# One order for 64 attentions: S0, S1, S2, C0, S3, C1, ..., C29, C30, C31, in a decoder layer on one NeuronCore

## What is computed

```python
x1 = layernorm(x + self_attention(x))         # 16 heads of 16, rotary embedding, no mask
x2 = layernorm(x1 + cross_attention(x1, ctx)) # 16 heads of 16, key mask, biases, out projection
gates = softmax(x2 @ router_w + router_b)     # 8 experts, top 2
```

## Time and profile before

| | us |
|---|---|
| median of 3 runs | 2200.92 (2197.92 to 2202.95) |
| the profiled execution | 2197.93 |
| its span in the profile | 2196.1 |
| h0 begins, h4 begins | 15.58, 102.42 |
| h61 begins | 1442.89 |
| last product with the values (C31) ends | 1577.02 |
| first matmul on rows of experts | 1606.36 |

### The profile page before, as it was taken

The page is one execution under the profiler, slowest core; times in us unless marked ns, Lnnn a source line. Parts: engine busy times, 40 slices in busy tenths (PEclk is TensorE's granted clock), DMA queues, the critical chain, the costliest instruction groups (busy, mean ns, idle before and its releaser), DMA issues. The chain is left out here.

```text
span 2196.1 us, 48374 instructions
## 1 busy us (share of the span) xinstructions
PE 2151.0 (98%) x18871; PEld 1498.1 (68%) x18877; DVE 1197.1 (55%) x2512; ACT 992.4 (45%) x1514; POOL 653.8 (30%) x1011
## 2 busy tenths in 40 slices
PE   8999999999999999999999999999999999999996
PEld 4566666666666666666666666666567877778785
DVE  3566776676776766776766776764411111111146
ACT  2355555555555555555555555555212122222233
POOL 2122233333233333233333233333221212121244
PEclk7899999999999999999999999999999999999998
DMA  3330101111100110000100000100023224331353
GB/s 109 101 114 31 36 32 50 55 43 52 53 27 27 36 34 30 28 22 25 31 31 27 28 24 23 33 29 19 13 60 80 39 63 89 80 73 32 84 209 158
DMA packets 96288, 117.01 MB, mean 53 GB/s; under 512 B 11360, under 2 KB 89005, under 8 KB 94016
## 3 DMA queue, kind: packets, MB, share of 16 engines
q1 hardware_dynamic: 66640, 82.37, 11.5%
q0 software_dynamic: 17184, 19.66, 4.9%
q10 hardware_dynamic: 12240, 11.88, 1.6%
HBM read 65.84 MB, written 56.05 MB: 56 GB/s over the span
## 5 line engine op out<-in xcount | busy, mean ns | idle before, releaser
L877 DVE TENSOR_REDUCE smax<-ps_s 128x4 f32<-128x1024 f32 x500 | 610.0, 1220 | 303.5 <-PE ps_s L577 264.0
L763 ACT ACTIVATE prob<-ps_e 128x1024 f32<-128x1024 f32 x500 | 512.0, 1024 | 497.6 <-PE ps_e L586 397.4
L577 PE MATMUL ps_s<-stack 17*128 17x256 f32 x4000 | 571.3, 403 | 14.8 <-DVE smax L877 9.1
L586 PE MATMUL ps_e<-stack 18*128 18x256 f32 x4000 | 567.6, 401 | 1.1 <-ACT prob L763 1.0
L577 PEld LDWEIGHTS ps_s<-stack 17*128 17x128 f32 x4000 | 346.6, 185 | 195.7 <-issue 104.1
L586 PEld LDWEIGHTS ps_e<-stack 18*128 18x128 f32 x4000 | 341.9, 184 | 5.9 <-issue 4.2
L1668 ACT ACTIVATE hid<-m_ps_h,b_sb 128x320 f32<-128x320 f32 x256 | 134.7, 527 | 392.2 <-PE m_ps_h L1622 392.2
L1622 PE MATMUL m_ps_h<-m_cols,w_sb 128*128 128x320 f32 x1024 | 290.7, 433 | 0.6 <-DVE m_cols L1691 0.6
L1639 PE MATMUL m_ps_o<-w_sb,hid 128*128 128x256 f32 x1280 | 279.1, 379 | 1.0 <-DVE m_res L1720 1.0
L1639 PEld LDWEIGHTS m_ps_o<-w_sb,hid 128*128 128x128 f32 x1280 | 243.1, 190 | 36.2 <-DVE m_res L1720 1.4
L602 PE MATMUL ps_w<-prob,val 128*32 128x256 f32 x4096 | 253.6, 389 | 0.2 <-ACT prob L763 0.2
(11 more groups left out here) (147 smaller groups left out, 2289.5 us busy)
## 6 DMA issues: line engine op xcount, KB each, us to landing
w_sb<-in_w SPq DMA_DIRECT2D x16, 1024.0 KB, 6.1
slot_rows_dram<-m_rows ACTq DMA_DIRECT2D x40, 258.0 KB, 2.6
m_rows<-slot_rows_dram SPq DMA_DIRECT2D x15, 645.0 KB, 4.2
xT<-in_xT SPq DMA_DIRECT2D x32, 256.0 KB, 2.8
ctxT<-in_ctxT SPq DMA_DIRECT2D x32, 256.0 KB, 2.8
x_res<-in_x SPq DMA_DIRECT2D x32, 256.0 KB, 2.7
sums_dram<-x SPq DMA_DIRECT2D x32, 256.0 KB
c_rows<-sums_dram SPq DMA_DIRECT2D x8, 1024.0 KB, 14.0
```

Of the source, the lines that this page charges most:

```text
L577: mm = nc.tensor.matmul(scores[:, p % 2, t, :], stack[X][rows, Q, p // HG, t * P:(t + 1) * P], stack[X][rows, K, p // HG, :], start=True, ...
L586: mm = nc.tensor.matmul(shifted[:, p % 2, t, :], stack[Y][rows, K, h // HG, t * P:(t + 1) * P], stack[Y][rows, Q, h // HG, :], start=True, ...
L763: nc.scalar.activation(prob[:, h:h + 2, :].rearrange("p h s -> p (h s)"), shifted[:, :, :, :].rearrange("p h t s -> p (h t s)"), ACT.Exp, ...
L877: nc.vector.tensor_reduce(max_columns(X, p), scores[:, :, :, :], AX.X, ALU.max)\
```

## The change

The 64 attentions get one written order, `items`, and half step h is: scores of item h, shifted scores of item h-1, output of item h-2, preparation of item h+1, and x2 and routing of a cross item at h-3 and h-4. Nothing is left out between the first and the last item, so there are 65 half steps with duos, 63 of them with two streams (h0 has S0's scores alone, h64 C31's shifted scores alone). S(b) comes at h(2b-2) from b = 3 on, C(b) stays at h(2b+3) up to C29, and C30 and C31 follow it at h62 and h63.

```diff
+        items = [(SELF, 0), (SELF, 1), (SELF, 2)]
+        for b in range(NB - 3):
+            items += [(CROSS, b), (SELF, b + 3)]
+        items += [(CROSS, NB - 3), (CROSS, NB - 2), (CROSS, NB - 1)]
+        rank = {item: k for k, item in enumerate(items)}
...
+        def side(at_item):
+            return rank[at_item] % 2
+        def fellow(at_item):
+            return item(rank[at_item] - 2)
...
+        def half_steps(emit, eng):
+            for h in range(2 * NB + 4):
+                emit(h, item(h), item(h - 1), item(h - 2), item(h + 1), item(h - 3), item(h - 4))
...
+        OUT_ROWS, X2_COLUMNS, COUNT, PROJECT_OUT, ROUTE, VALUES, EARLY_VALUES = 1, 3, 5, 6, 6, 7, 1
+        COLUMNS, STACK_K, STACK_Q = (4, 5), (5, 6), (6, 7)
+        LATE_STACK_K, LATE_STACK_Q = (6, 6), (7, 7)
+        PROJECT, LATE_PROJECT = ((2, 2, 3, 3), (2, 3, 5, 5)), ((3, 3, 4, 4), (3, 3, 5, 5))
...
-            spins_beside_one_stream = {
-                (last + 1, CROSS): (0, (0, 0, 2, 3, 3, 0, 0, 0)), (last + 2, SELF): (2, (2, 2, 3, 2, 0, 2, 1, 2)),
-            }
+            spins_beside_one_stream = {2 * NB: (2, (2, 2, 3, 2, 0, 2, 1, 2))}
...
+                    if s is not None and early(s) and m == EARLY_VALUES:
+                        values(*s, 0)
+                        values(*s, 1)
...
-                    n = (2 * i + X - 1) * DUOS + m
-                    if 0 <= n < EMPTY_PARTS:
-                        empty_rows(n)
+                    k = (h - 2) * DUOS + m
+                    if 0 <= k < EMPTY_PARTS:
+                        empty_rows(k)
...
+                settled = item(h - 5)
+                if is_of(CROSS, settled) and settled[1] < NB - 3:
+                    scatter(settled[1])
...
+                if is_of(CROSS, r):
+                    if p != (CROSS, NB - 1):
+                        place(r[1])
+                    if r[1] >= NB - 3:
+                        scatter(r[1])
```

More of the change, by code:

```diff
@@ L514, in project @@
                     take_bank("project", Y, b, half)
+                if n == 0 and Y == CROSS and b == 0:
+                    pe.wait_ge(load_w.sem, load_w.count(0))
                 if n == 0:
@@ L617, in columns @@
                 take_bank("columns", X, b)
-                rows = x1 if X == SELF else att2
+                rows = x1[b % 2] if X == SELF else att2
                 for k in range(KD):
@@ new lines, in emit @@
+                    if n is not None and m == slot_of(STACK_Q, LATE_STACK_Q, n):
+                        make_stack("stack_q", *n, 0)
+                    if is_of(CROSS, q) and m == ROUTE:
+                        route(q[1])
+                    if s is not None and not early(s) and m == VALUES:
+                        values(*s, 0)
+                        values(*s, 1)
+                    if h in spins_beside_one_stream:
+                        w, times = spins_beside_one_stream[h]
+                        if times[m] and w in held:
+                            steps_of, at_b, at_k = held[w]
+                            pe.wait_ge(steps_of.sem, steps_of.count(at_b, at_k))
+                        keep_warm(times[m], ps_w[:, w, :])
@@ L723, in _ @@
+                    if (h, m) in spins:
+                        pe.wait_ge(s_max[CROSS].sem, s_max[CROSS].count(NB - 1))
+                        pe.wait_ge(e_exp[CROSS].sem, e_exp[CROSS].count(NB - 1))
+                        keep_warm(spins[h, m])
             for n in range(4):
@@ L747, in stack_columns @@
                 act.wait_ge(tr_mm[Y].sem, tr_mm[Y].count(b, 2 * half + (1 if part == K else 2)))
-                if part == K and e_mm[Y].due(b - 1, 4 * half + 4):
-                    act.wait_ge(e_mm[Y].sem, e_mm[Y].count(b - 1, 4 * half + 4))
-                nc.scalar.copy(stack[Y][:, part, 2 * half:2 * half + 2, :],
+                other = fellow((Y, b))
+                if part == K and other is not None:
+                    act.wait_ge(e_mm[other[0]].sem, e_mm[other[0]].count(other[1], 4 * half + 4))
+                nc.scalar.copy(stack[side((Y, b))][:, part, 2 * half:2 * half + 2, :],
                                work(name, Y, half).rearrange("p (g s) -> p g s", g=2)).then_inc(tr_ev[Y].sem, 1)
```

450 lines of the change are left out of this document (220 added, 230 removed).

## The result

The changed kernel took 2194.72 us (median of 9 executions, 2191.57 to 2195.85), the kernel before, run in turn with it, 2201.12 (9, 2197.92 to 2202.95). The ratio is 0.9965, 95% interval 0.9956 to 0.9974, so 6.4 us less between the medians (5.7 to 9.7 by the interval of the ratio). The forecast was 2192 with an own range of 2187 to 2197. The profiled execution of the changed kernel is its median, 2194.72, with a span of 2192.9; that of the kernel before, 2197.93, was the fastest of its nine. The two profiles therefore differ by only 3.2 us.

The account below looks back on a forecast made before the run. PE, busy for 98% of the span, was taken to bound the kernel. Up to the last product -18.3 us, routing tail +7.0 and clock +2.0 summed to -9.3, giving 2192 us, own range 2187 to 2197.

Parts of the forecast that it names:

- Fewer half steps with one stream: Whole kernel: 16 single duos (-17.1 us) and eight spins (-2 us) go from PE's work.
- Front: Up to the start of h3: h3 starts at 86.3 us, a gain of 16.1 us.
- The upper bound of 96: Front: latest start forecast for h3, in us; the lower bound was 83.
- Rival 2: Front gives nothing extra, 2200 us: clock stays low in h0 (+6.4) and falls once more (+1.7); chance 0.23.
- The rule weighed: Clock in h0: activity releases the throttle early, so 2192 stands; with no release before h1, 2198.
- Middle: h3 to h60: 58 half steps of the same content as before, 1364.2 us, no gain taken.
- End: h61 to the last product: h61 and h62 together 59.7 us, h63 23.8, h64 21.8, last product with clock 2.9.
- Tail: Last product to the experts: three sets of scatters behind C31's deviation on GpSimd instead of two, +7.0 us.
- Clock at the experts' start: Start of the experts, after PE's last 50 spins: a fall of the clock, +2.0 us.
- rival 4: Middle gets shorter too, by up to 4.8 us, 2187 us; chance 0.07.
- rival 3: Slower, 2213 us: each gap opens a low stretch like the first one, 18.9 us at 0.51; chance 0.10.

Follow-up runs that it names:

- bank 1: Changed kernel with the early values (S0, S1, C29, C30) in bank 1 instead of bank 3: 2206.06 us, ratio 0.9992 to the kernel before.
- the first profile: Profiled execution of the changed kernel in the first measurement, no further edit, before the three groups of experiments: 2194.72 us.
- groups 1 and 2: First two of three experiment groups, each run with the kernel before in turn; the unedited changed kernel in group 2: 2203.88 us, ratio 0.9986.

## Why the prediction was right, and where it was off

- *Fewer half steps with one stream.* Right: from the first duo to the end of the last product the changed kernel took 1550.9 us, the kernel before 1561.4, at the same mean clock of 0.986, and the old order put back gives the old time.
- *Front.* The work and the waits were priced right, the clock was not: this is the step that failed. I had 70.7 us from the first duo to h3, 67.2 of them without falls (I took off 3.5). With the gaps filled it measured 68.7 and 67.6, in the changed kernel 78.5. So the clock cost 9.8 us against the first of these, and not 3.5: 1.0 because it rose at 23.3 us, where I had taken 21.1, and 8.8 behind that. I had priced the falls in h1 and h2 with 2.5 and 1.0, after the 1.7 of one slow product in h63; here a low stretch lasted 13.7 us, over duos, stacks, gaps and the values (6.8 to 17.1 in the other profiles without spins), and one began in h0, where I had seen no gap long enough (0.47 us). The upper bound of 96 held with 94.2. Rival 2 had the right size (+8.1, measured +7.9), for another reason: the clock did rise in h0. Its 6.4 us for a clock that stays low over 12.7 us of work was mis-reckoned besides: at the lower clock the duo took 2.08 instead of 1.13 us and the values 3.62 instead of 1.89, so such work costs nearly its own length again.
- *The rule weighed.* The Trainium skill, "TensorE: Matmul & The Clock Gate", section "What's actually happening", says that activity releases the throttle. By that rule 2192 stood, and the traces bear it out in part. In the ten profiles with the new order that show a low clock in h0, it rose at 19.1 to 23.3 us, from 1.5 us behind the start of S0's values to 1.8 us behind their end. But of three profiles with the old order only the first has the rise at the end of S0's values (34.1 us); in the other two it came at 43.3 and 43.9, although the values had taken 3.78 us from 31 us on. So the trace that I had read was a lucky one. Filling the gaps with work kept the clock up in the front. What made the time come out at 2194.7 is how easily it falls again.
- *Middle.* 1364.2 forecast, 1363.9 measured.
- *End.* h61 28.7 + 1.7 = 30.4, measured 30.40; h62 29.3 and 28.1; h63 23.8 and 23.75; h64 with the last product 24.7 and 26.3. Together 108.2 forecast (with 1.0 for the last product's clock) and 108.5. The waits of 1.64 us are there as named, and bank 1 shows what they cost, 2.5 us for the two. The parts are off by more than the sum (h62 at a clock of 1.00 had no fall, where I had put 1.7), so the 0.3 us is in part luck.
- *Tail.* +7.0 forecast, +6.9 measured to the first transposes, +7.1 to SyncE's load. The three sets did stand back to back on GpSimd (1576.75 to 1598.08), as forecast, and GpSimd's queue ended last: DVE had C31's positions ready at 1586.4, and GpSimd took them at 1589.9. But the queue is not all of it: 3.9 go with C30's scatters, and 3.2 are left even so, for DVE's later choice for C31. C29's set alone, the one that I had named as new, is worth 1.25.
- *Clock at the experts' start.* 2 us forecast, none in the first profile, 2.3 in the executions of groups 1 and 2 with 50 spins (idle 5.6 to 5.8 us), 0.3 in the one without C29's scatters (idle 6.3), none with 70 (1.4 to 1.5 us). It has the right size and comes in some executions.
- *Middle shorter (rival 4), each gap as long as the first (rival 3).* Rival 4 did not come. Rival 3 was nearer than I thought: two low stretches of 13.7 us in the front. But in the first profile the one in h61 lasted only 3.4 us (1470.5 to 1474.0), and none opened at the experts.

Summed: 8 us lost in the front against the forecast, 2 won at the experts, the rest within 1 us, gives the -3.2 of the profiles instead of -9.3. On the medians it is -6.4. That 2194.72 lies inside 2187 to 2197 is thus luck in part: two errors stood against each other (the front and the experts), and the fastest of the nine executions of before had been profiled, of the changed kernel the median. Profile to profile the forecast was off by 6 us. What stays open is how much of the difference between the two figures is the luck of one execution of the kernel before and how much its own falls; and why the gain was 0.14% on one chip and 0.35% on another is told by the stages of one profile each, not by repeated ones.

## What to carry to other kernels

An order with fewer half-empty steps packs the same waits into less time, so its gaps come closer together; that is how I read the front, no run shows it. Before timing such an order, list PE's gaps of half a microsecond and more, and fill them with spins in a free bank: here the order alone gave 0.35% and 0.14%, the order with its gaps filled 0.8%, and with more of them filled and bank 1 1.0%. How much of this the same spins would give in the old order was not tried; its front has low stretches too, so the 1.0% is not the order's. A wait that is taken away could only be timed once the clock was steady; until then read it in the trace. Where two queues follow each other in a tail, leave out one set at a time: the set that was added is not always the one that costs.

## What the runs showed of the hardware

- The granted clock fell to one half (1.2 of 2.4 GHz) at 33.5 us with PE busy for 2.53 of the 3 us before 33, behind an idle time of 0.47 us among duos of one stream and stacks; with four spins more in that stretch it did not. Busy time alone doesn't decide it: it stayed at 1.00 over 3 us with 2.21 busy in the changed kernel, and with 2.08 busy (57 to 60 us) in the one with spins in the front.
- With the same instructions the clock rose at 19.1 to 23.3 us in ten profiles. Behind 3.78 us of dense matmuls for the values it stayed low for another 8.6 and 8.9 us in two of three profiles with the old order.
- The clock of a stretch differs between executions of one kernel, and 0.001 of the mean over the kernel goes with about 2 us.
- On two of the chips each half step took 0.07 us longer at a granted clock of 1.00 and unchanged order, from about h8 on.
- In one execution nearly all matmuls took 1.7 to 1.9 times as long throughout, at a recorded clock of 1.00, while VectorE's reductions took 1.22 us as ever.
- Four scatters of GpSimd stand 1.27 to 1.42 us apart from start to start, with 0.90 us of waiting ahead of the first where it follows the slots directly.
